# Involution products by quarters of 32 channels, and a Gram matrix from tokens times inverse variance

## What is computed

```python
x = x + _L0_conv_ref(_gn(x), ...)      # involution, then projection wp
t = _to_tokens(x)
t = t + _L1_attn_ref(_ln_t(t), Wq, Wk, Wv, Wo)
t = t + _L1_ffn_ref(_ln_t(t), ...)
x = _from_tokens(t, x)

def _L1_attn_ref(emb, Wq, Wk, Wv, Wo):
    attn = jnp.einsum('bhnd,bhne->bhde', qh, kh)
    mu = attn.mean(axis=(2, 3), keepdims=True)
    var = attn.var(axis=(2, 3), keepdims=True)
    attn = (attn - mu) * jax.lax.rsqrt(var + EPS)
    attn = jax.nn.softmax(attn, axis=3)
    ctx = jnp.einsum('bhde,bhne->bhdn', attn, vh)
```

## Time and profile before

| | us |
|---|---|
| median of 3 runs | 71.14 (70.98 to 72.2) |
| the profiled execution | 71.06 |
| its span, first to last instruction | 69.2 |
| PE busy | 58.1 (84%) |
| DVE busy | 42.5 (61%) |
| ACT busy | 37.7 (55%) |
| POOL busy | 12.2 (18%) |
| mean granted clock of TensorE | 0.986 |

### The profile page before, as it was taken

The page is one execution under the profiler, slowest core; times in us unless marked ns, Lnnn a source line. Parts: engine busy times, 40 slices in busy tenths (PEclk is TensorE's granted clock), DMA queues, the critical chain, the costliest instruction groups (busy, mean ns, idle before and its releaser), DMA issues.

```text
span 69.2 us, 1689 instructions
## 1 busy us (share of the span) xinstructions
PE 58.1 (84%) x589; PEld 38.6 (56%) x596; DVE 42.5 (61%) x185; ACT 37.7 (55%) x88; POOL 12.2 (18%) x25
## 2 busy tenths in 40 slices
PE   3998997997999388899978399997999899999520
PEld 1313466995877345599756359593434433897100
DVE  3878927898778873152562824942636369479950
ACT  0623496570757954534389414899656433764810
POOL 6995170000982000000000000000000004400000
PEclk9999999999999999999999999999999999999995
DMA  0899967930000000000000000000000000000022
GB/s 1 230 381 237 243 205 201 211 52 0 0 9 0 5 0 0 0 0 0 9 0 0 0 0 5 9 0 0 0 0 0 0 0 5 0 9 0 0 73 78
DMA packets 5528, 3.40 MB, mean 49 GB/s; under 512 B 2896, under 2 KB 5072, under 8 KB 5520
## 3 DMA queue, kind: packets, MB, share of 16 engines
q1 hardware_dynamic: 5056, 2.59, 16.3%
q10 hardware_dynamic: 288, 0.44, 1.7%
q0 software_dynamic: 176, 0.27, 1.2%
HBM read 3.03 MB, written 0.26 MB: 48 GB/s over the span
## 4 chain that ended last, share of the span: by engine, by line
PE 43%; DVE 23%; ACT 15%; issue 8%; DMA 5%; DVEq 3%
PE ps L775 40%; DMA xg<-in_x 5%; ACT dsb L375 3%; DVEq L283 2%; ACT f L388 2%; ACT L462 2%; DVE w1s L716 2%; ACT e_sd L381 2%; DVE f_st L532 2%; PE ps L810 2%; ACT t L375 2%; DVE e_st L532 2%; DVE xp L601 1%; DVE gst L580 1%; DVE pv L676 1%
## 5 line engine op out<-in xcount | busy, mean ns | idle before, releaser
L775 PE MATMUL ps<-zeros 128*128 128x512 bf16 x63 | 20.2, 423 | 1.5 <-DVE zeros L574 1.2
L775 PEld LDWEIGHTS ps<-zeros 128*128 128x128 bf16 x70 | 6.4, 105 | 9.6 <-issue 4.2
L364 POOL TENSOR_TENSOR fb<-f,b2s 128x256 f32<-128x256 f32 x2 | 1.5, 735 | 37.9 <-DVE b2s L739 37.9
L775 PE MATMUL ps<-fT,w1s 64*128 64x256 f32 x16 | 5.5, 426 | 0.4 <-DVE w1s L716 0.3
L486 ACT ACTIVATE h<-ps,fb1T 128x256 f32<-128x256 f32 x8 | 3.8, 471 | 3.8 <-PE ps L775 3.8
L775 PE MATMUL ps<-wt,xw 128*64 128x128 f32 x64 | 4.5, 279 | 0.4 <-issue 0.4
L375 ACT ACTIVATE dsb<-ps 32x256 f32<-32x256 f32 x8 | 3.0, 376 | 2.3 <-PE ps L775 2.1
L775 PEld LDWEIGHTS ps<-wt,xw 128*64 128x64 f32 x64 | 3.5, 136 | 1.0 <-issue 0.6
L775 PEld LDWEIGHTS ps<-fT,w1s 64*128 64x128 f32 x16 | 2.4, 184 | 2.8 <-issue 1.9
L775 PEld LDWEIGHTS ps<-w2s,h 128*128 128x128 f32 x32 | 3.6, 192 | 0.3 <-ACT h L486 0.3
L775 PE MATMUL ps<-wpg,dsb 128*128 128x128 f32 x16 | 2.8, 298 | 1.2 <-ACT dsb L375 1.1
(11 more groups left out here) (178 smaller groups left out, 121.2 us busy)
## 6 DMA issues: line engine op xcount, KB each, us to landing
fw<-in_L_ffn_W SPq DMA_DIRECT2D x3, 256.0 KB, 4.2
wvT<-in_wvT SPq DMA_DIRECT2D x1, 260.0 KB, 4.5
xg<-in_x ACTq DMA_DIRECT2D x1, 256.0 KB, 3.4
x<-in_x SPq DMA_DIRECT2D x1, 256.0 KB, 4.0
wq<-in_L_attn_Wq SPq DMA_DIRECT2D x2, 128.0 KB, 4.0
wk<-in_L_attn_Wk SPq DMA_DIRECT2D x2, 128.0 KB, 4.3
fb<-in_L_ffn_b POOLq DMA_DIRECT2D x1, 256.0 KB, 4.4
out<-res SPq DMA_DIRECT2D x2, 128.0 KB, 1.7
```

The costliest lines, as they stand in the source:

```text
L364: pool.tensor_tensor(fb[:, 4 * i:4 * i + 4, :].rearrange("p (s l) c -> p s (l c)", s=NS), f[:, 4 * i:4 * i + 4, :].rearrange("p (s l) c -> ...
L775: return pe.matmul(dst, lhsT, rhs, start=start, stop=stop)
```

## The change

1. Products are made by quarters: `group_product` does 16 matmuls per tile, each for 32 channels and the two groups these hold (64 columns). A chunk d now holds both groups of a quarter side by side in 256 columns.
2. `read_product` goes. ACT multiplies the first group's columns by a 0/1 mask per partition (`part_of`) into `dhalf`; DVE multiplies the second group's by the other mask and adds `dhalf`, giving `dsb`. `project` is one matmul with the block matrix `wpb`.
3. Statistics are taken from the PSUM sum itself; ACT's copy to `t` waits for them. No square root is needed: `ts` is (t - mean) / (variance + eps), even half tiles on DVE, odd ones on POOL, and the Gram chunk adds t' ts. As `t` still has its mean, Wq and the means of Wk are centred by a matrix `cen` that POOL makes, PE applies and ACT and DVE copy (`wqz`, `wkz`).
4. One square root over all tiles, on ACT behind its Gram copy, and one product on POOL give `e` later; its four transposes stand on PE ahead of the value products, in place of a warm-up, and ACT copies `eT` after the exponentials.
5. `WARM["norm1"]` goes from 3 to 2.

```diff
-        ("gram", "V"), ("eT", "A"), ("gq0", "V"), ...
-    ("o0", "O"), ("o1", "O"), ("v00", "V"), ...
+    ("wqz", "A"), ("wkz", "V"), ("gram", "V"), ("gq0", "V"), ...
+    ("o0", "O"), ("o1", "O"), ("eT", "A"), ("v00", "V"), ...
...
+            def first_half(i):
+                act.wait_ge(dma["const"], 16)
+                wait_chunk(act, f"d{i}")
+                act.activation(dhalf[:, i, :].rearrange("p (h w) -> p h w", h=8), product_half(i, 0), ACT.Copy, scale=part_of[:, 0:1]).then_inc(made["half_products"], 1)
...
+            def second_half(i):
+                dve.wait_ge(made["half_products"], i + 1)
+                dve.scalar_tensor_tensor(dsb[:, i, :].rearrange("p (h w) -> p h w", h=8), product_half(i, 1), part_of[:, 1:2],
+                                         dhalf[:, i, :].rearrange("p (h w) -> p h w", h=8), ALU.mult, ALU.add).then_inc(read_v, 1)
...
-                    for l in range(2):
-                        ins = mm(dst[l * C:(l + 1) * C, j * P:(j + 1) * P], xw[:, t_, q, l * C:(l + 1) * C], wt[:, l, t_, q, :, :, :])
+                    for quad in range(P // QUAD):
+                        l, g = divmod(quad * GPAIR, G)
+                        r = slice(quad * QUAD, (quad + 1) * QUAD)
+                        ins = mm(dst[r, j * C:(j + 1) * C], xw[:, t_, q, r], wt[:, l, t_, q, :, g:g + GPAIR, :])
...
-                for g in range(GPAIR):
-                    ins = mm(bank(f"t{i}")[:, 0:P], dsb[:, g, t_, 8 * s:8 * s + 8, :], wpg[:, g, :, :], False, g == GPAIR - 1)
+                ins = mm(bank(f"t{i}")[:, 0:P], dsb[:, i, :], wpb[:, :, :], False, True)
...
+            mm(begin("wqz"), cen[:, :], wq[:, :]).then_inc(written, 1)
...
-                last = mm(gram_[:, t_ * P:(t_ + 1) * P], e[:, 2 * i:2 * i + 2, :], e[:, 2 * i:2 * i + 2, :], s == 0, s == NS - 1)
-                ins = pe.transpose(eT_[:, i * P:(i + 1) * P], e[:, 2 * i:2 * i + 2, :], ident)
+                ins = mm(dst[:, t_ * P:(t_ + 1) * P], t[:, 2 * i:2 * i + 2, :], ts[:, 2 * i:2 * i + 2, :], s == 0, s == NS - 1)
```

More of the change, by code:

```diff
@@ L355, in _ @@
             pool.tensor_scalar(wqm[:, :], wqs[:, :], 1.0 / C, None, ALU.mult).then_inc(made["wqm"], 1)
+            pool.wait_ge(dma["const"], 16)
+            pool.tensor_scalar(cen[:, :], blk, -float(C), None, ALU.mult).then_inc(made["centring"], 1)
+            pool.wait_ge(made["centring"], 1)
+            pool.tensor_tensor(cen[:, :], cen[:, :], ident, ALU.add).then_inc(made["centring"], 1)
             pool.wait_ge(made["wqm"], 1)
@@ L358, in _ @@
                                wqm[:, :].unsqueeze(2).to_broadcast([P, HEADS, C]), ALU.subtract).then_inc(made["wqc"], 1)
+            for i in range(NQ):
+                wait_read(pool, f"t{i}")
+                pool.wait_ge(made["e_inverse"], i + 1)
+                j = 2 * i + 1
+                pool.tensor_scalar(ts[:, j, :], t[:, j, :], norms["e"][1][:, j, 0:1], evr[:, j:j + 1], ALU.subtract, ALU.mult).then_inc(made["scaled_inputs_g"], 1)
+            pool.wait_ge(made["scaled_inputs"], NQ)
+            pool.wait_ge(made["scaled_inputs_g"], NQ)
+            pool.wait_ge(made["input_roots"], 1)
+            pool.tensor_tensor(e[:, :, :], ts[:, :, :], norms["e"][2][:, :].unsqueeze(2).to_broadcast([P, NT, C]), ALU.mult).then_inc(made["e"], 1)
             pool.wait_ge(made["f"], NQ)
@@ L432, in _ @@
             copy(gram[C:, :, C:], bank("gram")[C:, 0:BH * P].rearrange("p (t q) -> p t q", t=BH)[:, :, C:]).then_inc(made["gram_read_by_scalar"], 1)
-            wait_chunk(act, "eT")
-            copy(eT[:, :, :], bank("eT")).then_inc(read_a, 1)
+            act.wait_ge(made["input_variances"], NQ)
+            act.activation(norms["e"][2][:, :], ev[:, :], ACT.Sqrt).then_inc(made["input_roots"], 1)
             wait_chunk(act, "gq1")
@@ L448, in _ @@
             act.preload_act_table(ACT.Sqrt)
+            wait_chunk(act, "eT")
+            copy(eT[:, :, :], bank("eT")).then_inc(read_a, 1)
             act.wait_ge(const["m"], 1)
@@ L943, in _ @@
             mm(begin("o1")[:, 0:P], ident, t[:, 2:4, :], True, False).then_inc(written, 1)
-            keep_warm("v00", WARM["softmax"])
+            dst = begin("eT")
+            pe.wait_ge(made["e"], 1)
+            for i in range(NQ):
+                ins = pe.transpose(dst[:, i * P:(i + 1) * P], e[:, 2 * i:2 * i + 2, :], ident)
+            ins.then_inc(written, 1)
             pe.wait_ge(dma["wv"], 16)
@@ L1097, in front_layout @@
     f[:, F_GROUP:F_GROUP + P] = (p[:, None] % C == (p // C * GRP + p % C // 2)[None, :]) * -0.5
[L1098 removed]
+    wpb = np.zeros((2, C, 2, C), np.float32)
     for l in range(2):
[L1100 to L1103 removed]
+        wpb[l, :, l, :] = wp.T
+    return f, w2r, wpb.reshape(P, 2, C)
 def kernel(**inputs):
```

152 lines of the change are left out of this document (90 added, 62 removed), and 4 rows, old and new, of the table CHUNKS.

## The result

The kernel after takes 68.9 us where the one before takes 71.1: the ratio is 0.969, with a 95% interval of 0.964 to 0.974. The profiled execution of after took 68.93 us with a span of 67.1, against 71.06 and 69.2 in the one profiled before. The direction and the places were right; one term, the stretch up to the Gram copy, was sized 1.0 us too long.

The account below looks back on a forecast made before the run. The bound was taken as the chain through the product stage, ACT and DVE to DVE's Gram copy at 27.97. Sum: 71.06 - 1.5 (earlier copy) + 0.05 (transposes) + 0.40 (bank) = 70.0 us; range 69.3 to 71.4, likeliest case 69.7 to 70.4.

Parts of the forecast that it names:

- The products: Product matmuls on PE: 32 records per tile would cost 0.6 to 1.5 us, taken as 0.65.
- The halves: Masked product reads, in series: ACT's first half taken as 0.37 us, DVE's second half as 0.35.
- The tail of the Gram products: PE from Gram product 1 to the Gram copy: 1.30 plus 0.56 us, with warm-ups last, not DVE's scale 3.
- The transposes: Four transposes of normalised tokens ahead of the value products, replacing one warm-up: 0.66 us, counted as 0.05 later.
- The bank: o2 takes o0's bank, so PE waits for ACT's read of o0: 0.40 us later, passed on whole.
- The stop of PE: PE's "issue" stop from 16.50 to 16.90 us, after 9 records of the first product, was left where it is.
- the ring's length: One turn through DVE's second half, moments, statistics, ACT's token copy and next first half: 1.72 us.
- the tail: DVE's work behind the last second half (ends 22.02): inverses, moments, statistics, scales and small operations, to scale 1's end at 24.35.
- The shorter ring: Rival: ACT's half at 0.28 and DVE's at 0.29 us, each turn 0.15 shorter, 69.5 us; chance 0.20.
- The longer ring and the late GpSimd: Rival: ACT's half 0.46, PSUM statistics end to end (0.44), or POOL operations at 0.8 us; 70.6 us; chance 0.22.
- The instruction blocks: Rival: PE's instructions run out inside product 3, a block coming at 23 us, time 71.9; chance 0.10.
- The clock: Rival: PE's clock falls to 1.2 GHz over Gram and score products, adding 2 to 4 us, 73; chance 0.05.

Follow-up runs that it names:

- warm_one: The kernel after with one warm-up matmul between Gram products in place of two; 68.69 us.
- banks_free: The kernel after with o2 in bank 0, o3 in bank 2 and fsum in bank 5, so PE does not wait for ACT's read of o0 and o1; 68.77 us.
- early_22: The kernel after with 22 tiny matmuls (44 instructions with weight loads) put into PE's idle time ahead of its wait for xg; 71.42 us.
- products_only: The kernel before with the quarter products, masked reads and single projection, but the old normalisation, Gram matrix and banks; 71.08 us, ratio 1.002.
- loads_late: The kernel after with SP's issues of late-used loads (wvT, feed-forward weights and vectors) held back until DVE has done the last tile's statistics; 68.90 us.

## Why the prediction came out too high

**Right, by its numbers.** The products: 0.65 us for 32 records, taken from the row of four tiles, and it is 0.65. The halves: 366 ns on ACT for the 0.37 taken, 351 on DVE for 0.35. The tail of the Gram products behind scale 1: 1.86 from the start of product 1 to the copy, measured 1.87 (23.61 to 25.48), with the warm-ups ending last; warm_one shows that they do, by 0.25. The transposes: no cost; the weights for the value products load at 34.62, 2.47 earlier than the earlier trace rows, against 2.49 for the Gram copy. The bank: +0.40, measured +0.41 and shown by banks_free. The stop of PE stays where it was in the program: yes, and early_22 shows why.

**The step that failed: the ring's length.** It was put at 1.72 us, with the second halves 2 and 3 at 19.95 and 21.67. They came at 19.86 and 21.22: the first 0.09 early, the turn 1.36 long. The terms were each right as lengths (0.35, the aggregates, 0.33 for the 0.35, 0.28, 0.36). What was wrong was to add them. On one engine the next instruction's record starts before the last one's is over. In the timeline of after, DVE's second half (0.35) is followed 0.27 later by the first aggregate, the second comes 0.09 behind, the statistics 0.06 behind that: 0.42 from the second half to the statistics where the sum had 0.60. On ACT the copy (0.28) is followed 0.17 later by the first half: 0.11 less. Of the remaining 0.07, 0.04 is in the hand-overs (0.08 for the 0.12 taken) and 0.03 in the statistics and the half, at 0.33 and 0.36. The forecast allowed for an overlap of the two aggregates and for no other, though the timeline of before had it to be read:

```profile
21.66 0.35 DVE L532 BATCH_NORM_STATS2 e_st<-t 128x6 f32<-128x64 f32 x2
21.93 0.30 DVE L563 TENSOR_SCALAR e<-t,e_mv,e_sd 128x64 f32<-128x64 f32 x1
```

The statistics are 0.35 long, and the scale behind them starts after 0.27.

**The same mistake again in the tail.** From the start of the last second half to that of scale 1 the prediction had 2.38 (21.67 to 24.05); it is 1.97 (21.22 to 23.19): a dozen small DVE operations added at their lengths, while most start 0.06 to 0.12 behind the last. And the 0.2 added for statistics from PSUM and for double waits had no row behind it and cost nothing: the pair of statistics takes 0.33.

Together: 0.09 upstream, 0.36 in the ring, 0.41 in the tail and 0.20 of the allowance, less 0.08 for a scale 0.02 longer, a hand-over to PE 0.05 longer (23.51 to 23.61) and 0.01 in the Gram products: 0.98, against 0.97 from 26.45 to 25.48. The other 0.1 between 70.0 and 68.93 lies behind the copy, where 0.45 was added and 0.36 came.

**The rivals.** The shorter ring was the one that came, but for another reason than it gave: the halves cost what was taken, not less. Its 69.5 was too high as well, since it too added lengths. The longer ring and the late GpSimd did not come: GpSimd's scales took 0.615 us each, not 0.45, but they started at 22.07 and an end at 24.48 was early enough; it would have been the next bound, 0.25 away (warm_one). The instruction blocks did not run out before the last projection; the next packet moved at 17.95 and no idle above 0.3 us put down to "issue" stands between 17 and 26 on PE. The clock did not fall in the profiled execution of after, but products_only shows how near that was: half of the change alone lost it. The rule of the Trainium skill that the prediction weighed there (Runtime: NRT & Kernel Launch, Instruction fetch mechanics: the crossing of a block is mostly hidden) does not hold near 16 us in the kernels here whose own loads fill the DMA engines until 14.3 to 14.6 us, with 0.40 to 1.61 us of stop, and holds in loads_late, where the engines were free and PE did not stop.

**What the prediction left unasked.** It took the stop of 0.40 in the chain as given, and one wait on SyncE removes it. And it kept DVE and GpSimd apart except for one sentence on contention; the runs show that contention as a wait of 0.74 us (1.04 instead of 0.30) once the two meet.

## What to carry to other kernels

For a ring over several engines, add the distances from start to start that the timeline shows for such a pair, not the lengths of the records; the lengths are right only for the last operation ahead of another engine. When a part that should gain gives nothing, look at what ends at the same time as before, here DVE's scale 0 at 22.2 and GpSimd's last scale at 24.5, and move what holds it; edits that give next to nothing apart may give more together. A stop put down to "issue" with the instruction queue at work is worth a test by holding back the loads that are wanted last; and a few instructions more ahead of such a stop, even in idle time, can be dear.
